# Feed-forward input turned by VectorE on a way through DRAM, instead of by TensorE

## The reference, cut to what matters

```
h = _layernorm(x) * (1 + ca) + sa
x = x + ga * attention(h)
h = _layernorm(x, axis=-1) * (1 + cb) + sb      # cb, sb: one number per feature
gate = jnp.einsum('bsd,hd->bsh', h, wg)
up = jnp.einsum('bsd,hd->bsh', h, wu)
x = x + gb * jnp.einsum('bsh,dh->bsd', jax.nn.silu(gate) * up, wd)
```

## Time and profile before

| | |
|---|---|
| Time, median of 3 runs | 2003.87 us (2003.59 to 2005.35) |
| The profiled execution's own time | 2005.31 us |
| Its span | 2003.5 us |
| Attention ends at about | 1007 us |
| A feed-forward group | 124.8 us |
| Busy: PE / PEld / DVE / ACT / POOL | 1961.1 / 1592.4 / 1439.8 / 906.2 / 873.5 us |

### The profile page before, as it was taken

One profiled execution on the slowest core, in us unless ns is written; L12 is line 12 of the kernel. 1 busy time (PEld: TensorE's weight loads), 2 busy tenths in 40 slices (PEclk: granted clock), 3 DMA queues, 4 the chain that ended last, 5 costly groups with the idle time before them and its releaser, 6 DMA issues. The chain is left out here.

```text
span 2003.5 us, 43850 instructions
## 1 busy us (share of the span) xinstructions
PE 1961.1 (98%) x16008; PEld 1592.4 (79%) x16008; DVE 1439.8 (72%) x2386; ACT 906.2 (45%) x1542; POOL 873.5 (44%) x718
## 2 busy tenths in 40 slices
PE   7999999999999999999899999999999999999999
PEld 4788888888888888887678888888888888888887
DVE  7977887877888877787875857658576585765744
ACT  5444444344444344444254536445364453644533
POOL 2533544444544444443334444444434444344444
PEclk9999999999999999999999999999999999999999
DMA  7223333444433434433475654656546565465553
GB/s 268 66 94 102 112 122 122 127 135 129 121 117 123 133 122 134 130 101 96 158 282 176 209 172 150 226 168 209 175 146 224 169 210 184 144 215 171 169 169 106
DMA packets 202521, 309.81 MB, mean 155 GB/s; under 512 B 16145, under 2 KB 72977, under 8 KB 202386
## 3 DMA queue, kind: packets, MB, share of 16 engines
q1 hardware_dynamic: 201858, 306.78, 48.0%
q10 hardware_dynamic: 528, 1.05, 0.1%
HBM read 225.19 MB, written 82.58 MB: 154 GB/s over the span
## 5 line engine op out<-in xcount | busy, mean ns | idle before, releaser
L1496 POOL TENSOR_TENSOR h_lo<-y_rows,h_hi 128x512 fp32r<-128x512 f32 x192 | 246.6, 1304 | 369.1 <-ACT h_hi L1594 369.0
L461 POOL TENSOR_TENSOR x_res<-y,x_res 128x512 f32<-128x512 f32 x64 | 82.9, 1296 | 293.9 <-DVE y L872 283.4
L851 DVE TENSOR_TENSOR probs<-sc,causal 128x512 f32<-128x512 f32 x256 | 158.3, 680 | 3.9 <-PE sc L1155 2.9
L612 ACT ACTIVATE z_exp<-pj,qk_neg 128x512 f32<-128x512 f32 x128 | 88.0, 687 | 161.5 <-PE pj L1136 159.1
L1136 PE MATMUL pj<-xt_hi,w_hi 128*128 128x512 f32 x512 | 146.3, 407 | 12.0 <-DVE a_t L861 10.8
L1924 PE MATMUL sc<-wd,h_hi 128*128 128x512 f32 x384 | 150.7, 392 | 0.0
L450 POOL TENSOR_TENSOR a_lo<-a_t,a_hi 128x512 fp32r<-128x512 f32 x60 | 82.4, 1373 | 154.5 <-ACT a_hi L626 154.5
L1924 PE MATMUL sc<-wd,h_lo 128*128 128x512 f32 x384 | 149.6, 390 | 0.0
L1136 PE MATMUL pj<-xt_lo,w_hi 128*128 128x512 f32 x512 | 138.8, 393 | 1.7 <-DVE xt_lo L789 1.7
L1136 PE MATMUL pj<-xt_hi,w_lo 128*128 128x512 f32 x512 | 138.2, 392 | 0.0
L1709 DVE TENSOR_TENSOR r_den<-pj,k_tok 128x512 f32<-128x512 f32 x96 | 66.2, 690 | 98.3 <-ACT k_tok L1577 52.6
(11 more groups left out here) (248 smaller groups left out, 5386.5 us busy)
## 6 DMA issues: line engine op xcount, KB each, us to landing
w_hi<-parts SPq DMA_DIRECT2D x48, 1024.0 KB, 5.4
w_lo<-parts SPq DMA_DIRECT2D x48, 1024.0 KB, 5.3
x_mid<-x_res SPq DMA_DIRECT2D x96, 256.0 KB, 2.9
x_res<-in_L_attn_x SPq DMA_DIRECT2D x64, 256.0 KB, 2.8
k_dram<-k_block SPq DMA_DIRECT2D x252, 64.0 KB, 1.8
xg<-in_L_attn_x SPq DMA_DIRECT2D x15, 1024.0 KB, 7.6
x_res<-x_mid SPq DMA_DIRECT2D x60, 256.0 KB, 4.0
full<-x_mid SPq DMA_DIRECT2D x60, 256.0 KB, 3.6
```

What stands on the lines that cost most here:

```text
L461: pool.tensor_tensor(out=x_res[:, slot, :], in0=y[:, :], in1=x_res[:, slot, :], op=ALU.add).then_inc(y_ready, 1)
L612: act.activation(z_exp[:, n % 2, :], pj[:, n % 2, :], ACT.Relu, bias=qk_neg[:, 1 - kind, c:c + 1], scale=-scale).then_inc(below_ready, 1)
L851: dve.tensor_tensor(out=probs[:, h, :].rearrange("p (c i) -> p c i", c=C), in0=sc[:, h, :].rearrange("p (c i) -> p c i", c=C), in1=causal[ ...
L1496: pool.tensor_tensor(out=h_lo[b], in0=h[i], in1=h_hi[b].bitcast(F32), op=ALU.subtract).then_inc(h_lo_ready, 1)
```

## The change

TensorE's turns go. The normalised x of a half group (512 tokens, 1 MB) is written by SyncE to a DRAM tensor `xn_dram` and read back into the same buffer by four DMAs of 256 KB, one for each set of 32 partitions. A piece of 512 bytes (128 features of one token) lands on a partition, 16 x 128 numbers to a partition and half. VectorE's `transpose` then turns every 32x32 block of the 128x2048 buffer in place: one instruction a half, two a group. Features then lie on the partitions in an order of their own; the columns of the gate and up weights and the modulation are regrouped to it when the inputs are laid out. ScalarE's `evacuate` reads the turned blocks from SBUF with a stride instead of a PSUM bank. The normalisation moves some steps ahead. Group 0 keeps attention's turns, so its x is brought into the same order by the load: each of the two half loads becomes 16 DMAs with pieces of 128 bytes.

```diff
+                for t in range(GT):
+                    for c in range(C):
+                        sp.dma_start(xg[:, t, c * P:(c + 1) * P].rearrange("p (h e) -> p h e", h=HPC),
+                                     mid_groups[half, :, t, :].rearrange("p (h c e) -> c p h e", h=HPC, c=C)[c]
+                                     ).then_inc(x_in, 16)
-                sp.dma_start(xg[:, :, :], mid_groups[half, :, :, :]).then_inc(x_in, 16)
...
+        def save_xn(G, second):
+            wait(sp, xn_ready, G * 4 + (2 * second - 2))
+            sp.dma_start(xn_dram[second * GN:(second + 1) * GN, :].rearrange("(t p) d -> p t d", p=P),
+                         xg_halves[second][:, :, :]).then_inc(xn_out[second], 16)
+
+        def load_blocks(G, second):
+            wait(sp, xn_out[second], G * 16)
+            for h in range(HPC):
+                sp.dma_start(xg_halves[second][h * E:(h + 1) * E, :, :].rearrange("p t (b x) -> p (t b) x", x=P),
+                             xn_dram[second * GN:(second + 1) * GN, h * P:(h + 1) * P].rearrange("(b i) x -> i b x", i=E)
+                             ).then_inc(xb_in[second], 16)
...
+                    first = isinstance(G, int) and G == 0
+                    if not last and q == (6 if first else 5):
+                        save_xn(G + 1, 0)
                     if not last or q + 4 < HB:
                         load_parts(G, q + 4)
+                    if not last and q == (7 if first else 6):
+                        save_xn(G + 1, 1)
+                    if not last and first and q == 7:
+                        load_blocks(G + 1, 0)
+                    if not last and q == (8 if first else 7):
+                        load_blocks(G + 1, 1)
...
                     store(G, i)
+                    if i == 1 and not last and not (isinstance(G, int) and G == 0):
+                        load_blocks(G + 1, 0)
...
-        def evacuate(G, i, bank):
+        def evacuate(G, i):
-            wait(act, xt_ps, G * 8 + (i - 7))
+            wait(act, xt_ps, G * 2 + (second - 1))
-            act.activation(to, bank, ACT.Identity, bias=mod_col[:, SB, c:c + 1],
+            turned = xg_halves[second][:, :, :].rearrange("p t (b c i) -> p c (t b) i", c=C, i=E)[:, c, :, :]
+            act.activation(to.rearrange("p (b i) -> p b i", i=E), turned, ACT.Identity, bias=mod_col[:, SB, c:c + 1],
...
+        def turn(G, second):
+            wait(dve, xb_in[second], G * (16 * HPC))
+            blocks = xg_halves[second][:, :, :].rearrange("p t d -> p (t d)")
+            dve.transpose(blocks, blocks).then_inc(xt_ps, 1)
...
-                if ahead and not first and 2 <= q < 6:
-                    norm_stats(G + 1, q - 2)
-                if ahead and q == 5:
+                if ahead and not first and 1 <= q < 5:
+                    norm_stats(G + 1, q - 1)
+                if ahead and q == (5 if first else 4):
                     norm_var(G + 1)
-                if ahead and 7 <= q < 10:
-                    norm_x(G + 1, q - 6)
+                if ahead and not first and q == 5:
+                    norm_x(G + 1, 0)
+                    norm_x(G + 1, 1)
...
+                if ahead and (q - 9 if first else q - 8) in (0, 1):
+                    turn(G + 1, q - 9 if first else q - 8)
...
-        def turn(G, i, bank):
-            wait(pe, xn_ready, G * 4 + (2 * second - 2))
-            for t in range(GT):
-                mm = pe.transpose(bank[:, t * P:(t + 1) * P], xg[second * GT + t][:, c * P:(c + 1) * P], ident[:, :])
-            mm.then_inc(xt_ps, 1)
```

More of the change, by code:

```diff
@@ L43 @@
 Signals = namedtuple("Signals", "wide_ready wd_in xt_ps xf_ready a_ready y_gated y_ready y_out xr_ready state_ready op_ready pj_ready part_out b_ready sum_made b_high")
-Shared = namedtuple("Shared", "xg xf h_hi h_lo ring b_hi b_lo full wd silu_sum saved gate h y x_res gb_row pairs sums dn")
+Shared = namedtuple("Shared", "xg xg_halves xf h_hi h_lo ring b_hi b_lo full wd silu_sum saved gate h y x_res gb_row pairs sums dn")
 Turned = namedtuple("Turned", "kt qt v r_den probs prod k_block k_sum a_hi a_lo")
@@ L143, in build @@
                                       x_mid, k_dram, parts, downs)
-        ffn = feed_forward(sem, later, ident, mod_col, half_neg, norm, gb_dram, parts, att, shared, x_mid, out)
+        ffn = feed_forward(sem, later, mod_col, half_neg, norm, gb_dram, parts, att, shared, x_mid, xn_dram, out)
         block = top.enter_context(nc.Block())
@@ L259, in attention @@
     flat_diag = kv_diag[:, :, :].rearrange("p c f -> p (c f)")
-    shared = Shared([xg[:, t, :] for t in range(GT)] + [z[:, i, :] for z in (z_exp, z_relu) for i in range(2)],
+    shared = Shared([xg[:, t, :] for t in range(GT)] + [z[:, i, :] for z in (z_exp, z_relu) for i in range(2)], [xg, z],
                     [xf[:, 0, :], xf[:, 1, :], r_den[0][:, 0, :], r_den[0][:, 1, :]],
@@ L754, in norm_stats @@
         def norm_stats(g, tiles=range(GT)):
-            wait(dve, x_in, 16 * (g + 1))
+            wait(dve, x_in, 16 * (g + 1) if not isinstance(g, int) or g < NG else 16 * (NG + GT * C * (g - NG + 1)))
             for t in tiles:
@@ L1320, in attention, with feed_forward @@
     return Programs(sync, gpsimd, scalar, vector, tensor), signals, shared
-def feed_forward(sem, later, ident, mod_col, half_neg, norm, gb_dram, parts, att, shared, x_mid, out):
+def feed_forward(sem, later, mod_col, half_neg, norm, gb_dram, parts, att, shared, x_mid, xn_dram, out):
     stats, mean_var, var_eps, rstd = norm[1:5]
-    xg, xf, h_hi, h_lo, (blocks, filled), b_hi, b_lo, full, wd, total, saved, gate, h, y, x_res, gb_row, xs, sums, dn = shared
+    xg, xg_halves, xf, h_hi, h_lo, (blocks, filled), b_hi, b_lo, full, wd, total, saved, gate, h, y, x_res, gb_row, xs, sums, dn = shared
     c11, c12, c22 = total
@@ L1335, in feed_forward @@
     xt_ps, xf_ready = sem("fxt_ps"), sem("fxf_ready")
+    xn_out, xb_in = [sem(f"xn_out{i}") for i in range(2)], [sem(f"xb_in{i}") for i in range(2)]
     gb_in, gb_chain, gb_done = sem("gb_in"), sem("gb_chain"), sem("gb_done")
@@ L1398, in load_x @@
             else:
-                wait(sp, xt_ps, (G - 1) * 8)
+                wait(sp, xf_ready, (G - 1) * 8)
             for t in range(FT // 2):
@@ L1510, in body @@
             for q in range(HB):
+                if ahead and q == (5 if isinstance(G, int) and G == 0 else 4):
+                    rstd_of(G + 1)
                 if q not in (5, 11):
@@ L1622, in body @@
             for q in range(7, HB):
-                step(G, q, (lambda i=q - 9: evacuate(G + 1, i, dn[i])) if ahead and q >= 9 else nothing)
+                step(G, q, (lambda i=q - 9: evacuate(G + 1, i)) if ahead and q >= 9 else nothing)
             if not ahead:
@@ L1635, in body @@
             high(G + 1, T4, 0)
-            for i, bank in ((4, sums[0]), (5, sums[1]), (6, xs[0]), (7, xs[1])):
-                evacuate(G + 1, i, bank)
+            for i in range(4, 8):
+                evacuate(G + 1, i)
             for op in (B11, B21, T1, T2, B22, T3, T4):
@@ L1793, in body @@
             if ahead:
-                norm_x(G + 1, 0)
+                for pair in range(2) if isinstance(G, int) and G == 0 else range(2, 4):
+                    norm_x(G + 1, pair)
             for q in range(7, HB):
@@ L2020 @@
 _TURNED = ("L0_c",)
+REGROUPED = np.arange(D).reshape(HPC, C, E).transpose(1, 0, 2).reshape(D)
 def word_blocks(w_gate, w_up, w_down):
[L2024 removed]
+    w_gate, w_up = (np.asarray(w)[:, REGROUPED].reshape(HB, P, C, P).transpose(0, 2, 3, 1) for w in (w_gate, w_up))
     units = [np.concatenate([w_gate[j, k], w_gate[j, k + 2], w_up[j, k + 2], w_up[j, k]], axis=1)
@@ L2048 @@
         if name == "L0_wmod":
-            layouts.append(("in_wmod_t", a.T))
+            turned = np.ascontiguousarray(a.T).reshape(6, D, D)
+            for m in (SB_MOD, CB_MOD):
+                turned[m] = turned[m, REGROUPED]
+            layouts.append(("in_wmod_t", turned.reshape(6 * D, D)))
         for label, a in layouts:
```

37 lines of the change are left out of this document (9 added, 28 removed).

## The result

The changed kernel takes 2082.5 us (median of 4 runs, 2081.38 to 2086.53) against 2003.73 for the kernel before: ratio 1.0392, 95% interval 1.0380 to 1.0404, slower by 79 us where +7.7 was forecast and 2021 was the upper end. The page's first part of the changed kernel, the answer to the earlier trace rows: TensorE's busy time has hardly changed while the span grew from 2003.5 to 2081.0, so the loss is mainly waiting.

What follows compares the result with a forecast made beforehand. TensorE, 98% busy, was taken as the bound, with VectorE about level at a group's end. Turns -6.5, second half's read-back +7.2, group 0 +4, handover +3 gave +7.7 on 2005.31: 2011.6 us in the median, range 1998 to 2021.

Steps and rivals of the forecast that it cites:

- The sign: Whole kernel: the change makes it slower, +7.7 us; chance of slower 0.55.
- the step named as decisive: Second half's read-back in six loop groups: data 0.3 or 2.0 us late, a loss of 7.2 us.
- The read-back of the second half: Step 9's transpose in six loop groups waits 1.2 us a group for its data: loss 7.2, bounds 0 and 12.
- Rival 3: Slower still: reads at 225 GB/s and 128-byte pieces at their pace, 17.5 us lost, 2021.4; chance 0.14.
- The first half's read-back: Between two residual loads, delaying a GpSimd residual chain that is not the bound: costed at nothing.
- the case without cover: First half's read-back: if its cover is gone, `add_c11(6)` is late by the 1 MB, some 3 us a group.
- Group 0: Group 0's read-backs, queued behind weight loads, arrive late for steps 9 and 10: loss of 4 us, bounds 0 and 5.
- The handover: From attention: sixteen issues at 0.44 us delay the second half's statistics; loss of 3 us, bounds 0 and 7.
- The removed turns: TensorE's feed-forward turns: only three of eight a group count, 0.93 us a group, gain 6.5; bounds 0 and 20.2.
- VectorE's transposes: In middle steps 8 and 9: 2.29 us each (2.7 at most), hidden if their data is there.

Runs made afterwards that it cites:

- experiment 2: Changed kernel without the DRAM write and read-back, transposes kept, handover half loads one issue each again: 1995.77 us, ratio 0.9952.
- experiment 1: Changed kernel without the DRAM write and read-back; VectorE's transposes and the sixteen handover issues stay: 2004.47 us, ratio 0.9998.
- experiment 12: As experiment 11, but group 0's second-half x is reordered DRAM to DRAM a group earlier and loaded by one plain DMA: 1999.52 us, ratio 0.9970.
- experiment 3: Changed kernel with the four read-backs in 2 KB rows, still 32 partitions each: 2071.58 us, ratio 1.0335.
- experiment 4: Changed kernel with the four read-backs in 512-byte pieces, each covering all 128 partitions: 2039.57 us, ratio 1.0177.
- experiment 10: As experiment 9, but reads dealt out so both queues work in the same half of the partitions: 2019.62 us (one run).
- experiment 9: Changed kernel with transfers reordered earlier; SyncE reads into partitions 0 to 63, ScalarE's own queue into 64 to 127: 2016.59 us, ratio 1.0075.
- experiment 11: Changed kernel with transfers reordered earlier, and group 0's transposes and ScalarE's copies a step later: 2003.5 us, ratio 1.0003.

## Why the prediction was wrong

The sign was right and the step named as decisive was the one that decided; its size was a seventh of what was measured, and two terms set to nothing or to little were large.

**The read-back of the second half** (7.2 forecast; 49 measured beyond experiment 2, the 36 us of waiting and the 13 behind it). The data was forecast to be wanted 12.95 us after the start of step 8; by TensorE's wait of 6.79 it was wanted at 13.2. It was forecast at 13.25 to 14.95 and came at 19.96 (step 8 starts at 1489.26 in the changed kernel). Three parts of that failed. First the pace of the read: I took the middle between the stores of the earlier trace rows at 340 and at 225; the read ran at 150 to 210, below the slower end, although the row that resembled it (32 partitions) was on the table. A read into 32 partitions belonged at or below the 32-partition row, and "the reads together touch all partitions" was no reason for more: they run one behind another. Rival 3 had the right mechanism and too small a price. Second the landing times: 5.3 us for a weight load was the median of a queue without the new transfers. With them the load of block 10 took 7.6, so that the write, 2.6 behind it as forecast, was done at +8.6 instead of +6.25, and the weight load of block 11 took 9.2. It landed at +14.1 instead of +10.25, and the data came 5.9 behind it instead of 3.0 to 4.7. So of the 5.9 us beyond the middle of the forecast the landing made 3.8 and the pace 2.0, though the two are not wholly apart: the end of that load ran beside the read. Third, the consequence of a wait: I priced a late microsecond as one microsecond. In the group shown 6.8 us without matmuls also brought 1.5 us of lower clock.

**The first half's read-back** (0 forecast; some 18 us in the loop groups, 11 in the first halves' down tiles and some 7 in the products behind them). "A residual chain on GpSimd that is not the bound" was the step that failed: the chain is not the bound, but `gate_y` waits for it and `add_c11(6)` stands behind `gate_y`. VectorE's timeline of the kernel before already had both:

```profile
1313.15 0.69 DVE L1735 TENSOR_TENSOR a_t<-sc,ga_row 128x512 f32<-128x512 f32 x1 [1.69 <-POOL x_res L1501]
1314.57 0.69 DVE L1703 TENSOR_TENSOR r_den<-pj,k_tok 128x512 f32<-128x512 f32 x1 [0.72 <-PE pj L1867]
```

The second row is `add_c11(6)`. It ends at 1315.26, and TensorE wants it at 1317.99: 2.7 us of cover, which the late residual used up. The price that I named for the case without cover, some 3 us a group, was right.

**Group 0** (4 forecast): its second half took 9.4 longer than before, or 10.7 longer than in experiment 1. Same mistakes, same sign.

**The handover** (3 forecast, 8.7 measured). An issue was priced at 0.44 us by the `k_dram` row. SyncE's and VectorE's timelines of the changed kernel:

```profile
964.92 11.19 SPq L407 DMA_DIRECT2D xg<-x_mid  x16
```

```profile
978.37 1.29 DVE L762 BATCH_NORM_STATS2 stats<-xg 128x6 f32<-128x512 f32 x2 [8.28 <-DMA xg<-x_mid]
```

An issue took 0.70 us, so sixteen took 11.2 instead of 7.1. The upper bound of 7 had been worked out from the transfer's pace; the issues were the slower part. The first half's load was taken as hidden; VectorE's statistics waited 1.1 us for it, the other part of the 9.4 above.

**The removed turns** (6.5 forecast, 9.5 measured). The mechanism held: the turns beside VectorE's chain are worth nothing and TensorE waits 1.22 for `gate_y`. Four turns count instead of three; the chain itself became 0.6 shorter in experiment 2 (25.82 to 25.21 from its first sum to `add_c11`).

**VectorE's transposes** were right: 2.30 us against 2.29, and no cost of their own. The rule of the Trainium skill that was weighed against the change ("VectorE: DVE Perf Modes", Rules for kernel authors) did not decide here: without the way through DRAM the kernel with VectorE's transposes is 9.5 us faster than the one with TensorE's, and with the whole way, in experiment 12, some 5.

Another page would have given the pace. The Trainium skill, "SBUF — State Buffer", section Door 1, has a DMA into partitions 0 to 31 reach half of the ways into SBUF and 0 to 63 the same half, with 189 and 196 GB/s measured for 1 MiB against 328 for all 128. Experiments 3 (190 to 240), 4 (290 to 350) and 10 (190 to 200) agree in the pace for 32 partitions, for 128, and for 32 and 32 in the same half. The same page of the Trainium skill, section "Can I just issue two DMAs to hit both halves?", has two DMAs at a time into different halves gain only 6%; experiment 9, with 215 to 290 against the one queue's 155 to 210, does not agree.

What stays open: why a weight load behind these reads takes up to twice its time (shared queue or shared way in). In the loop groups it took 7.7 to 11.4 us there, and behind experiment 4's reads over all partitions, in the same queue, 5.3 to 8.9; that speaks for the way in, but the reads of 4 were also done sooner. A version of 12 without the first half's sixteen issues was not tried. The traces place a cost there: VectorE's step from one `k_block` transpose to the next beside these issues takes 15.3 us in experiment 1 (912.51 to 927.79) and 12.6 in experiment 2, with one issue (912.28 to 924.88), and it is 13.9 in 11 and 15.6 in 12.

## What to carry to other kernels

Price a transfer by the partitions that it touches before its bytes or pieces, and by the row of the same form even if that row is only a peak. A wait that an engine off the bound takes on is passed along to whatever stands behind it in program order: follow it until an engine is reached that nobody waits for. When a new transfer is late, move it before making it faster: the same slow bytes cost 78 us in one order and almost nothing in another (experiment 11).

## What the runs showed of the hardware

Reads into 32 partitions ran at 155 to 210 GB/s in 512-byte pieces (changed kernel) and mostly at 190 to 240 in 2 KB rows (experiment 3); reads of 512-byte pieces into 128 at 290 to 350 (experiment 4); two queues at a time at 215 to 290 in different halves of the partitions (experiment 9) and at 190 to 200 in the same (experiment 10). In the changed kernel a DMA of 512 pieces of 128 bytes kept SyncE 0.70 us, one of 512 pieces of 512 bytes 0.48 (1.92 for four).
